# A two-layer graph network with routed experts: gather chunks of 124 edges in place of 128

## The reference

```python
def gcn_conv(x, W, b, src, dst, n_nodes):
    s, d = concatenate([src, loop]), concatenate([dst, loop])
    deg = segment_sum(ones, d)
    dinv = where(deg > 0, rsqrt(deg), 0.0)
    norm = dinv[s] * dinv[d]
    msg = (x @ W)[s] * norm[:, None]
    return segment_sum(msg, d) + b          # rows of the sources, summed by destination

out = relu(batch_norm(gcn_conv(layernorm(x), W1, b1, ...)))
out = batch_norm(gcn_conv(out, W2, b2, ...))
x = x + relu(out + layernorm(x))
x = x + experts(layernorm(x))               # router, top 2 of 6 experts, three matmuls each
```

## Time and profile before

| | |
|---|---|
| median of 3 runs | 7011.63 us (6996.64 to 7022.28) |
| the profiled execution, first to last instruction | 7009.1 us |
| POOL busy | 3732.7 us, 53% |
| PE busy | 3014.7 us, 43% |
| DVE busy | 1748.0 us, 25% |
| ACT busy | 840.1 us, 12% |
| DMA, mean over the span | 121 GB/s |

### The profile page before, as it was taken

One profiled execution on the slowest core, in us unless ns is written; L12 is line 12 of the kernel. 1 busy time (PEld: TensorE's weight loads), 2 busy tenths in 40 slices (PEclk: granted clock), 3 DMA queues, 4 the chain that ended last, 5 costly groups with the idle time before them and its releaser, 6 DMA issues. The chain is left out here.

```text
span 7009.1 us, 91724 instructions
## 1 busy us (share of the span) xinstructions
PE 3014.7 (43%) x24826; PEld 1994.5 (28%) x24827; DVE 1748.0 (25%) x6367; ACT 840.1 (12%) x1732; POOL 3732.7 (53%) x3810
## 2 busy tenths in 40 slices
PE   3333333333333334433333333333333443676675
PEld 3222222222222222322222222222222332444443
DVE  9611111111111112511111111111112543222221
ACT  5400000000000000500000000000001542222221
POOL 0266666666666665466666666666664343333333
PEclk5555555555555555555555555555555656888887
DMA  3754444444444443544444444444444343333332
GB/s 90 236 158 133 130 132 133 132 132 132 134 131 132 132 133 109 163 132 134 131 131 132 134 132 133 130 133 130 132 131 114 118 129 106 55 54 53 52 54 45
DMA packets 359556, 847.33 MB, mean 121 GB/s; under 512 B 70751, under 2 KB 183617, under 8 KB 359490
## 3 DMA queue, kind: packets, MB, share of 16 engines
q0 software_dynamic: 254848, 708.96, 38.0%
q1 hardware_dynamic: 104642, 137.62, 6.6%
HBM read 736.62 MB, written 109.69 MB: 121 GB/s over the span
## 5 line engine op out<-in xcount | busy, mean ns | idle before, releaser
L595 POOL DMA_INDIRECT ring<-messages,idx_stage x3328 | 3155.0, 948 | 1944.0 <-PE ps L1579 915.9
L1579 PE MATMUL ps<-onehot_mem,ring 128*128 128x64 bf16 x19968 | 1578.1, 236 | 2874.5 <-DMA ring<-messages,idx_stage 2187.5
L1579 PEld LDWEIGHTS ps<-onehot_mem,ring 128*128 128x128 bf16 x19968 | 1130.9, 123 | 3416.3 <-DMA ring<-messages,idx_stage 2073.1
L1099 DVE TENSOR_TENSOR acc<-acc,ps 128x128 f32 x832 | 240.3, 289 | 3968.9 <-PE ps L1579 2911.3
L650 POOL DMA_INDIRECT out_dram<-acc x216 | 333.4, 1543 | 767.3 <-DMA out_dram<-acc 602.2
L735 ACT ACTIVATE idx_stage<-tables 128x8 int32 (+1 forms) x416 | 86.5, 208 | 4785.8 <-PE ps L1579 3733.8
L1088 DVE TENSOR_SCALAR onehot_mem<-iota_bf,tables 128x64 bf16<-128x64 bf16 x3336 | 600.7, 259 | 105.6 <-issue 81.6
L1612 PE MATMUL ps<-acc,wconv 128*128 (+1 forms) x448 | 346.6, 930 | 245.6 <-DVE rows_mem L1130 194.2
L1807 PE MATMUL ps<-acc 128*128 128x256 f32 x864 | 314.5, 543 | 309.1 <-issue 309.1
L1795 PE MATMUL ps<-acc 128*128 128x512 f32 x864 | 381.7, 595 | 1.3 <-ACT acc L906 1.3
L1807 PEld LDWEIGHTS ps<-acc 128*128 128x128 f32 x864 | 241.7, 287 | 404.6 <-issue 351.6
(11 more groups left out here) (246 smaller groups left out, 2242.2 us busy)
## 6 DMA issues: line engine op xcount, KB each, us to landing
ring<-messages,idx_stage POOLq DMA_INDIRECT x3328
acc<-routed_rows SPq DMA_DIRECT2D x54, 520.0 KB, 3.7
rows_mem<-in_x_dram SPq DMA_DIRECT2D x62, 448.0 KB, 4.2
messages<-dinvT SPq DMA_DIRECT2D x28, 672.0 KB, 5.8
out_dram<-rows_mem SPq DMA_DIRECT2D x28, 448.0 KB
dinvT<-in_x_dram SPq DMA_DIRECT2D x22, 448.0 KB, 4.6
messages<-ring SPq DMA_DIRECT2D x14, 672.0 KB, 3.9
messages<-rows_mem SPq DMA_DIRECT2D x14, 672.0 KB, 3.9
```

What stands on the lines that cost most here:

```text
L595: pool.indirect_dma_start(out=slots[:, s, :], out_offset=None, in_=t_dram[layer], in_offset=bass.IndirectOffsetOnAxis(ap=idx_stage[:, u, s ...
L1099: dve.tensor_tensor(sums(w, WIN), sums(w, WIN), partial(u, WIN), ALU.add).then_inc(ev_fast[run], 1)
L1579: last = pe.matmul(ps[:, 2 * u + k, 0:width], slots[:, s, n * D + k * P:n * D + (k + 1) * P], onehot[:, ohu, j, 0:width], start=j == 0 and ...
```

## The change

`EC` becomes 124. A group has 496 edges. The gathers write partitions 0 to 123 of a slot and take 124 indices. The tables of destinations and sources are filled for 124 partitions; `rel3` (the destination within its window) and `dstT_i` are set to -1 first, so that rows 124 to 127 match no destination. Partitions 96 to 127 of `ring` are set to zero once, between the use of `ring` for degrees and the first gather. The products still read all 128 partitions.

```diff
-EC = P
+EC = 124
@@ gather
-                            out=slots[:, s, :], out_offset=None, in_=t_dram[layer],
-                            in_offset=bass.IndirectOffsetOnAxis(ap=idx_stage[:, u, s:s + 1], axis=0),
+                            out=slots[0:EC, s, :], out_offset=None, in_=t_dram[layer],
+                            in_offset=bass.IndirectOffsetOnAxis(ap=idx_stage[0:EC, u, s:s + 1], axis=0),
@@ scalar: sources, index stages
-                last = act.activation(src3[:, n * P:n * P + ng, :], turned[:, 0:ng, :], ACT.Copy)
+                last = act.activation(src3[0:EC, n * P:n * P + ng, :], turned[0:EC, 0:ng, :], ACT.Copy)
-                    act.activation(idx_stage[:, u, :], srcidx[:, bass.ds(i * (2 * SLOTS) + u * SLOTS, SLOTS)],
+                    act.activation(idx_stage[0:EC, u, :], srcidx[0:EC, bass.ds(i * (2 * SLOTS) + u * SLOTS, SLOTS)],
@@ vector: set-up
+            dve.memset(rel3, -1.0)
+            step(dve.memset(dstT_i, -1))
             dve.wait_ge(edges_in, 32)
-                    last = dve.tensor_copy(table[:, n * P:n * P + ng, :], turned[:, 0:ng, :])
+                    last = dve.tensor_copy(table[0:EC, n * P:n * P + ng, :], turned[0:EC, 0:ng, :])
+            dve.wait_ge(dinv_ready, 1)
+            dve.wait_ge(dn_in, 16)
+            step(dve.memset(ring[P // 4 * 3:P, :], 0.0))
             dve.wait_ge(dn_turned, 1)
@@ tensor
-                        last = turn(ps[:, bank + n, j * P:(j + 1) * P], table[:, n, j * P:(j + 1) * P])
+                        last = turn(ps[0:EC, bank + n, j * P:(j + 1) * P], table[:, n, j * EC:(j + 1) * EC])
```

## The result

The changed kernel takes 7775.55 us (median of 4 runs, 7771.34 to 7779.8) against 7006.92 us before (4 runs, 6996.64 to 7022.28): ratio 1.1094, 95% interval 1.108 to 1.1108. It is slower, as forecast, and inside the range of 7350 to 10,000; the forecast of 7430 us is 346 us too low. The range holds it because it was drawn to take in a rival, the dearer instruction; the forecast's own case ended at 7510.

What follows compares the result with a forecast made beforehand. POOL was taken to set the pace mostly, at 1.25 us a gather plus pauses waiting for PE. 7009.1 + 424 (more gathers) + 11.6 (set-up) - 14.3 (layer ends) = 7430 us, 6% slower; range 7350 to 10,000.

Steps and rivals of the forecast that it cites:

- the forecast's own case: Whole kernel: 124 rows divided near evenly among DMA engines, instruction at 0.949 us; 7430 us, range 7355 to 7510, chance 0.42.
- the dearer instruction: POOL's gathers: fewer engines make the instruction cost 1.542 us, about 8650 us in all; chance 0.24, 0.04 of it above 10,000.
- More gathers: Gather loops: 128 more gathers a layer, 53 with real edges and 75 padding; +212 us a layer, +424 us in both.
- The 53 real chunks: Gather loops: added chunks with real edges cost 1.489 us each, pauses included; +79 us a layer.
- The padding: End of each layer: 75 more gathers, all of row 0, at 1.77 us each (bounds 1.489 and 2.22); +133 us a layer.
- 124 rows in a gather: POOL's gathers: fewer bytes gain nothing, rows divide near evenly, eight on most engines, and the instruction stays at 0.949 us.
- The pauses: POOL's waits for PE after twelve gathers: 796 us in both layers, some 2.7 us each, on top of 1.25 us a gather.
- Fewer engines, longer way: Gathers on fewer DMA engines land later, 2.0 us longer, and each pause grows by this; chance 0.18.
- Faster: POOL's gathers: the instruction costs by the engines served, so fewer engines make the kernel faster; chance 0.13.
- No net change: Gather loops: one-row gathers could be cheap in a long run and pauses shrink, making up 424 us; chance 0.03.
- Set-up and tail: Before the first gather +11.6 us (degree steps, `ring` memset, table operations); node chunks behind the loop -14.3 us in both layers.
- The node chunks behind the loop: End of a layer: two node chunks fewer behind the loop, 3.57 us each; -14.3 us in both layers.

Runs made afterwards that it cites:

- count_only: The changed kernel with its 448 groups a layer and the padding, but gathers of 128 rows; 7415.23 us, ratio 1.0578 to the kernel before.
- the sweep of rows: The changed kernel with 120, 125, 126 or 122 rows a gather, 448 groups each; 7437.86, 7494.84, 7490.84 and 9133.49 us.
- slow_long: The kernel before with one POOL memset of 128 x 560 float32 behind each gather; 7762.78 us, ratio 1.0961.
- rows125: The changed kernel with 125 rows a gather, again 448 groups; 7494.84 us, ratio 1.0692 to the kernel before.
- rows122: The changed kernel with 122 rows a gather, again 448 groups; 9133.49 us, ratio 1.2893 to the kernel before.

## Why the prediction was right in its direction and wrong in its time

**The books before.** The stated range of the forecast's own case, 7355 to 7510, is its terms (7430 - 42 - 25 and 7430 + 68) rounded outward. Its terms leave 2053 + 11.6 - 14.3 = 2050 us for all that is not gathers, measured 2052. With the measured price of the gathers that gives 2050 + 3584 x (1.292 + 0.30) = 7756 us; the span is 7772.2.

**More gathers.** Right. The forecast had 7430 us for the count with the set-up and the tail; count_only, which is just that, took 7415.23. The 53 real chunks a layer were put at 1.489 us, and outside the padding the gathers of count_only's first layer take (2675 - 118) / 1717 = 1.489. The padding was put at 1.77 and takes 118 / 75 = 1.573, so that term is 150 x 0.20 = 30 us too high: three gathers at the end of a layer are no sample for a run of 75. In the changed kernel the padding costs nothing extra, since 1.60 is over 1.573.

**124 rows in a gather.** This step failed: "For the forecast I take the division as near to even as it can be, eight rows on most engines, and the instruction at 0.949 us." The division is 4 x 31 and the instruction takes 1.292 us. The argument for independence was that 112 and 128 rows cost the same. Both rows were read rightly, but they could say nothing on this: these are 7 and 8 rows on 16 engines (by the packets before, one of four rows and one of three on each for 112, two of three and one of two for 128), so the engines did not change and the rows on the fullest one moved by one, which is 0.013 us by the line above, and 0.004 measured. The prediction's last sentence named this mark rightly: the duration of the instruction is what differs.

**The pauses.** The forecast kept 0.24 us of them a gather, since it put the real chunks at 1.489 us, "pauses included". They are gone. I had read the earlier trace rows as a pause that is added to whatever the pace is, as long as one gather takes from issue to the end of its product. This step failed too. That way got 2.2 us longer (below), and the pauses went to nothing. The runs show a floor for the mean instead: the 0.343 us of the dearer instruction first ate the 0.24 us. The two failed steps pull in opposite directions. Without pauses to lose, the instruction alone would have added 3584 x 0.343 = 1229 us, so that the forecast is only 346 us too low is in part luck. Of the 764 us, the count explains 256 x 1.489 = 381, and the rest is 3584 x (1.596 - 1.489) = 383 us.

**The rivals.** No row of the kernel before shows how 124 rows are divided. That they sit on four engines, as the chances of 0.18, 0.24 and 0.13 and with them the range's end at 10,000 suppose, was an assumption, and the packets of the changed kernel bear it out. "Fewer engines, dearer instruction" is what happened, without pauses. That the price goes by the rows on the fullest engine, 31 in place of 8, is borne out by the sweep of rows and the packets. The rival's own price was that of the accumulating DMA, 1.542 us, and its time 2050 + 3584 x (1.542 + 0.30), about 8650 us. It is 0.25 us too high for the instruction; in proportion to the rows, 0.949 x 31 / 8 = 3.68 us, it would have been further off. It had 0.24 against 0.42 for the forecast, though nothing in the trace spoke for an even division either. "Fewer engines, longer way" had the longer way right, and its price too: a gather of 128 rows keeps each engine busy 0.47 x 1.489 = 0.70 us for eight rows, 0.0875 us a row, so 23 rows more are 2.0 us. The kernel's first gather is issued at 295.3 us before and at 305.6 in the changed kernel. The products, with the start of the first and the last:

```profile
L1579 PE MATMUL ps<-onehot_mem,ring x19968: 189/242/261, 298.8 to 5395.8; 128*128 128x64 bf16 x200
```

```profile
L1584 PE MATMUL ps<-onehot_mem,ring x21504: 189/242/261, 311.4 to 6170.4; 128*128 128x64 bf16 x200
```

That is 3.5 us from issue to product, and 5.8. Counted over the chunks with real edges of the first layer, the median is 3.15 us before and 5.34 in the changed kernel: 2.2 us longer, where the rival had 2.0. It isn't the pace, since slow_long has 3.11. With 5 engines (rows125) it is 4.78, with 2 (rows122) 8.72, so about 0.105 us for each further row of the fullest engine. But the rival let each pause grow by this, and there were none. Without them, eight slots at 1.60 us are 12.8 us ahead and hide it, so it cost nothing.

"Faster", where the instruction costs by the engines served, is out: on four engines it takes 1.292 us, on 16 it took 0.949. "No net change" had one of its two parts right, the pauses, but not enough.

**Set-up and tail.** First gather forecast at 295.3 + 11.6 = 306.9 us, measured 305.6. The degree steps cost what was said, 1.15 us each for eight more; the memset of `ring` takes 2.6 us, not 1.8:

```profile
190.00 2.62 DVE L1189 MEMSET ring<- 32x3072 f32 x1 [1.42 <-issue]
```

The node chunks behind the loop still follow each other at 3185.43 - 3181.85 = 3.58 us. The memset was off by 0.8 us and the node chunks by 0.01, and neither matters.

## What to carry to other kernels

Choose the rows of an indirect DMA by their divisors before their number: 112 and 128, multiples of 16, had the cheapest instruction here (0.945 and 0.949 us), and a few rows less can cost more than they save (122 rows take 1.67 us, 120 take 0.98, 128 take 0.95). A price that was read from two sizes says nothing about a third if the quantity that may set it hardly moved between the two; ask what each candidate (rows, engines, rows on an engine) was in both. And where an engine has a steady pace broken by pauses, don't add the pauses to a changed pace: ask whether the mean has a floor, which a filler instruction on that engine can show, if it is long enough to move the pace.

## What the runs showed of the hardware that was not expected

- The price of a gather on POOL follows the rows of the fullest DMA engine, about 0.013 us for each (8 rows 0.984, 25 rows 1.211, 61 rows 1.668), and with it goes the number of packets: 352 for a gather of 122 rows, of which 280 are of 12 bytes and 30 of 4, and 64 for one of 128.
- Gathers on four engines each keep POOL's pace here (its 468 waits for PE are the usual 0.30 us), but each gather lands later. The mean DMA share in the gathers is 0.45 to 0.46, and it was 0.47 to 0.48. Four engines out of 16 could not bear more than 0.25 (the large packets alone are 0.39), so successive gathers must take different ones. From issue to product a gather takes 5.34 us in place of 3.15, which eight slots hide.
- Gathers that all read one row load the DMA engines to 0.87 in place of 0.48, at 1.573 us a gather of 128 rows; that is no more than 0.08 us above the others, though each then takes 10.4 us from issue to product (median in count_only).
- The gap of 0.30 us between two gathers absorbs ten empty instructions or a memset of 0.12 us at no change of the pace (1.25 us).
- PE's signal that a product is done can stand in the records 8.3 us behind the product's end, with three more in 0.23 us; at a pace of 1.70 us between gathers no two signals come within 0.1 us of each other.
